# Attention scores issued as one step of four 32-row tiles into four PSUM banks, with unrolled programs and a new order of steps on every engine

## The reference, cut to what matters

```python
# layer 0: 32 heads of 16, 8 key/value heads, 128 queries and 128 keys per batch element
scores = einsum('bkgld,bksd->bkgls', q, k) * scale + mask
out = einsum('bkgls,bksd->bkgld', softmax(scores), v)
x = layernorm(out @ Wo + bo + x) * gamma + beta
# layer 1
xn = ln(x); sx = shift(xn)
xxx = tanh((xn + sx * maa_x) @ maa_w1)             # low
x5 = xn + sx * (maa_stack + xxx @ maa_w2)          # low_rank, mix: five inputs
w = exp(-exp(td + tanh(x5[1] @ decay_w1) @ decay_w2)); r, k, v, g = projections of x5
for t: out_t = r_t . (u * a_t + s);  s = a_t + w_t * s,  a_t = outer(k_t, v_t)   # 32 heads of 16x16
x = x + (groupnorm(out) * g) @ Wo.T
x = x + sigmoid(xr @ Wr.T) * (relu(xk @ Wk.T) ** 2 @ Wv.T)    # after a second ln and shift
```

## Time and profile before

| what | value |
|---|---|
| median of 3 runs | 2512.75 us (2511.68 to 2516.52) |
| the profiled execution | 2511.9 us |
| its span | 2510.1 us |
| PE busy | 2306.4 us, 92% |
| DVE busy | 2164.8 us, 86% |
| ACT busy | 942.2 us, 38% |
| POOL busy | 568.3 us, 23% |

### The profile page before, as it was taken

One profiled execution on the slowest core, in us unless ns is written; L12 is line 12 of the kernel. 1 busy time (PEld: TensorE's weight loads), 2 busy tenths in 40 slices (PEclk: granted clock), 3 DMA queues, 4 the chain that ended last, 5 costly groups with the idle time before them and its releaser, 6 DMA issues. The chain is left out here.

```text
span 2510.1 us, 43786 instructions
## 1 busy us (share of the span) xinstructions
PE 2306.4 (92%) x14144; PEld 1578.5 (63%) x14144; DVE 2164.8 (86%) x5337; ACT 942.2 (38%) x3169; POOL 568.3 (23%) x762
## 2 busy tenths in 40 slices
PE   4697999999999999999999999999999999999966
PEld 3474766667576675757657575665757666675633
DVE  1368999999989898998989889898898999999993
ACT  2434352624425252442624335262342526244111
POOL 1122223131222313122131212213122231322200
PEclk8798999999999999999999999999999999999977
DMA  7000001010000101001010100101001010100000
GB/s 249 19 10 29 1 10 37 2 46 1 19 29 10 38 1 46 1 10 38 10 37 1 39 9 10 38 10 37 1 14 34 10 37 4 44 1 20 8 17 9
DMA packets 48435, 61.86 MB, mean 25 GB/s; under 512 B 20208, under 2 KB 25968, under 8 KB 48208
## 3 DMA queue, kind: packets, MB, share of 16 engines
q1 hardware_dynamic: 48208, 58.93, 7.5%
HBM read 42.14 MB, written 16.78 MB: 23 GB/s over the span
## 5 line engine op out<-in xcount | busy, mean ns | idle before, releaser
L1140 DVE TENSOR_TENSOR_SCAN st<-ws,st 128x256 f32<-128x256 f32 x1024 | 620.5, 671 | 10.5 <-POOL st L994 10.4
L851 ACT ACTIVATE probs_or_mixes<-probs_or_mixes,least 128x128 f32<-128x128 f32 x1024 | 396.8, 397 | 25.1 <-DVE least L1087 24.6
L1150 DVE TENSOR_TENSOR st<-st,rT 128x1024 f32<-128x1024 f32 x256 | 327.5, 1280 | 19.4 <-issue 16.6
L1129 DVE TENSOR_TENSOR st<-bank_pair,kT 128x1016 f32<-128x1016 f32 x256 | 309.8, 1210 | 37.1 <-PE bank_pair L701 36.3
L1087 DVE CUSTOM_DVE_ANT_0 probs_or_mixes<-bank,nmask 128x128 f32<-128x128 f32 x1024 | 228.8, 285 | 55.8 <-PE bank L569 34.1
L1018 POOL TENSOR_TENSOR probs_or_mixes<-probs_or_mixes 128x512 f32<-128x512 f32 x160 | 187.4, 1193 | 268.0 <-DVE probs_or_mixes L1212 268.0
L1024 POOL TENSOR_TENSOR rstd<-rstd,mhalf 128x1 f32<-128x1 f32 x96 | 80.1, 835 | 701.4 <-DVE rstd L1169 701.4
L701 PE MATMUL bank_pair<-v_hi,sel 32*128 32x256 f32 x1024 | 187.3, 346 | 50.1 <-DVE st L1129 50.0
L994 POOL COPY st<-s 128x8 f32<-128x8 f32 x256 | 76.5, 312 | 646.3 <-PE bank L724 423.9
L851 ACT ACTIVATION_READ_ACCUMULATOR probs_or_mixes<-probs_or_mixes,least 128x1 f32 x1024 | 201.0, 196 | 0.0
L701 PEld LDWEIGHTS bank_pair<-v_hi,sel 32*128 32x128 f32 x1024 | 110.2, 189 | 131.3 <-DVE st L1129 70.9
(11 more groups left out here) (137 smaller groups left out, 4210.4 us busy)
## 6 DMA issues: line engine op xcount, KB each, us to landing
cin<-in_ctx SPq DMA_DIRECT2D x16, 512.0 KB, 3.7
xin<-in_x SPq DMA_DIRECT2D x16, 512.0 KB, 3.7
x<-xin SPq DMA_DIRECT2D x16, 512.0 KB, 3.7
keep<-x SPq DMA_DIRECT2D x16, 512.0 KB, 3.9
out<-keep SPq DMA_DIRECT2D x32, 256.0 KB, 2.0
wo<-in_wo SPq DMA_DIRECT2D x2, 1024.0 KB, 11.4
nmask<-in_mask SPq DMA_DIRECT2D x16, 128.0 KB, 4.5
wq<-in_wq SPq DMA_DIRECT2D x1, 1024.0 KB, 9.5
```

The lines of the kernel that those rows point to most:

```text
L851: last = fn(pr[:, n % 4, j, :], pr[:, n % 4, j, :], ACT.Exp, bias=least[:, n, j:j + 1], scale=-1.0, accum_out=rsum[:, n, j:j + 1])
L1129: tt(dst, src, over(kv, DU, 1), ALU.mult).then_inc(outer.sem, 1)
L1140: last = nc.vector.tensor_tensor_scan(v, ws[:, c].rearrange("p b t -> p (b t)"), v, 0.0, ALU.mult, ALU.add)
L1150: tt(v, v, over(rT[:, u // PER, :], DU, 1), ALU.mult).then_inc(weighed.sem, 1)
```

## The change

PE's score step now serves four tiles: it waits for the four banks of the ring at once and issues eight matmuls, four row groups in turn for each of the two column halves. DVE and ACT keep a step for each tile. The hardware loops are gone: all 18 iterations are written out on every engine. The four lists are in a new order. Instructions, their number and their sizes are the same.

```diff
@@ psum_jobs @@
         elif name == "score":
-            keys = [(name, n), (name, n + 1)]
+            keys = [(name, n + m) for m in range(4)]
@@ periods (the same on SP) @@
-            for it in range(LOOP_FROM):
-                once(it)
-            with eng.Fori(LOOP_FROM, LOOP_TO) as i:
-                once(i)
-            for it in range(LOOP_TO, G + LATEST):
+            for it in range(G + LATEST):
                 once(it)
@@ score on PE @@
+                four = range(n, n + 4)
                 hold(pe, emptied, g, *([through("key", 0)] if n == 0 else []),
-                     *([through("query", n // 4)] if n in (0, 4) else []), (("score", n), 0, 0),
-                     (("score", n + 1), 0, 0))
-                ps = {m: (bank[XB.of(("score", m))], filled[XB.of(("score", m))]) for m in (n, n + 1)}
+                     *([through("query", n // 4)] if n < 8 else []), *((("score", m), 0, 0) for m in four))
                 for ci in range(2):
-                    for m in (n, n + 1):
+                    for m in four:
+                        at = XB.of(("score", m))
                         r = slice(32 * (m % 4), 32 * (m % 4) + 32)
-                        last = mm(ps[m][0][:, ci * 2 * L:(ci + 1) * 2 * L], qT[r, 2 * cp + ci, b, :],
+                        last = mm(bank[at][:, ci * 2 * L:(ci + 1) * 2 * L], qT[r, 2 * cp + ci, b, :],
                                   kbd[r, b, :, :], start=True, stop=True)
                         if ci == 1:
-                            last.then_inc(ps[m][1], 1)
+                            last.then_inc(filled[at], 1)
@@ PE_ORDER, one line of ten @@
-low_rank.2+1 spread.14+2 tdecay.0+1 turn_c.0 proj_k.0+1 turn_c.1 spread.15+2 decay.0+1 turn_x.0 reduce.6+2 proj_v.0+1
+spread.15+2 low_rank.0+1 reduce.6+2 low_rank.2+1 proj_r.0+1 proj_k.0+1 proj_v.0+1 tdecay.0+1 turn_x.0 spread.0+1
```

More of the change, by code:

```diff
@@ new lines @@
+reduce.7+2 turn_c.0 decay.0+1 spread.1+1 mean.1+2 decay.1+1 var.0+2 turn_x.1 proj_r.1+1 turn_c.1 spread.2+1 query.0
+key.0 rstd.0+2 rstd.1+2 query.1 low_rank.4+1 spread.3+1 out.0+2 reduce.0+1 score.0 spread.4+1 out.1+2 proj_k.1+1
+proj_g.0+1 proj_g.1+1 turn_p.0 spread.5+1 turn_p.1 turn_p.2 score.4 reduce.1+1 spread.6+1 turn_m.0+2 turn_p.3 value.0
+proj_v.1+1 turn_p.4 turn_m.1+2 spread.7+1 values.0 turn_p.5 turn_p.6 turn_p.7 score.8 spread.8+1 reduce.2+1 ffn_k.0+2
+spread.9+1 values.1 flip.0 turn_p.8 turn_p.9 turn_p.10 share.0 score.12 reduce.3+1 turn_p.11 project.0 spread.10+1
@@ L130 @@
+turn_p.12 turn_p.13 values.2 ffn_k.1+2 turn_p.14 ffn_r.0+2 flip.1 turn_p.15 share.1 spread.11+1 values.3 reduce.4+1
+spread.12+1 project.1 spread.13+1 ffn_v.0+2 spread.14+1 ffn_r.1+2 turn_n.0 turn_n.1 reduce.5+1 ffn_v.1+2 mean.0+1
+low.0
 """
 ACT_ORDER = """
-turn_c.0 turn_x.0 turn_c.1 decay.0+1 proj_v.0+1 turn_x.1 proj_r.0+1 decay.1+1 mean.1+2 proj_r.1+1 query.0 key.0
-proj_g.0+1 proj_v.1+1 score.0 score.1 score.2 proj_g.1+1 query.1 turn_p.0 turn_p.1 score.3 turn_p.2 score.4 turn_p.3
-score.5 score.6 turn_p.4 turn_p.5 score.7 proj_k.1+1 turn_p.6 turn_p.7 flip.0 score.8 score.9 share.0 score.10
@@ L139 @@
+score.10 ffn_k.0+2 flip.0 turn_p.8 turn_p.9 turn_p.10 share.0 score.11 turn_p.11 score.12 score.13 score.14 score.15
+turn_p.12 ffn_k.1+2 turn_p.13 turn_p.14 flip.1 turn_p.15 ffn_r.0+2 share.1 ffn_r.1+2 turn_n.0 turn_n.1 mean.0+1 low.0
+proj_r.0
 """
 POOL_ORDER = """
-rk.0+1 first.1+1 rk.1+1 negate.0 mix.4+1 first.2+1 first.3+1 first.4+1 norm2.0+2 first.5+1 turn_x.0 first.6+1
-norm2.1+2 turn_x.1 rk.2+1 first.7+1 norm0.0 first.8+1 first.9+1 affine0.0 norm1.0 norm0.1 affine0.1 rk.3+1 first.10+1
@@ L149 @@
[L149 to L152, removed]
-score.10 score.11 scan.6+1 score.12 score.13 scan.7+1 gather.0 score.14 outer.8+1 score.15 shift2.0+2 project.0
@@ L154 @@
-inverse.1 weigh.6+1 norm0.0 weigh.7+1 scan.8+1 apply0.0 outer.9+1 gather.1 weigh.8+1 scan.9+1 norm1.0 project.1
-norm0.1 weigh.9+1 apply0.1 keep_row.0 outer.10+1 readout.1+1 apply1.0 norm1.1 outer.11+1 apply1.1 scan.10+1
-weigh.10+1 shift.0 outer.12+1 scan.11+1 scan.12+1 weigh.11+1 ffn_v.0+2 ffn_v.1+2 mix.0 mix.1 outer.13+1 mix.2 mix.3
+proj_v.0+1 weigh.15+2 outer.0+1 readout.3+2 outer.1+1 var.0+2 scan.0+1 outer.2+1 weigh.0+1 groupnorm.0+2 scan.1+1
+scan.2+1 weigh.1+1 mix.4+1 out.0+2 outer.3+1 score.0 score.1 norm2.0+2 score.2 score.3 scan.3+1 weigh.2+1 weigh.3+1
@@ new lines @@
+outer.4+1 apply2.0+2 out.1+2 scan.4+1 norm2.1+2 weigh.4+1 proj_g.0+1 proj_g.1+1 outer.5+1 apply2.1+2 score.4 score.5
+score.6 outer.6+1 score.7 scan.5+1 scan.6+1 value.0 proj_v.1+1 readout.0+1 weigh.5+1 outer.7+1 weigh.6+1 shift2.0+2
+score.8 score.9 score.10 score.11 key.0 outer.8+1 inverse.0 scan.7+1 scan.8+1 weigh.7+1 gather.0 score.12 score.13
+outer.9+1 score.14 scan.9+1 score.15 outer.10+1 project.0 readout.1+1 weigh.8+1 inverse.1 scan.10+1 norm0.0 weigh.9+1
+apply0.0 weigh.10+1 outer.11+1 gather.1 norm1.0 outer.12+1 scan.11+1 project.1 norm0.1 apply0.1 keep_row.0 apply1.0
@@ L157 @@
+outer.13+1 weigh.11+1 norm1.1 ffn_v.0+2 apply1.1 scan.12+1 shift.0 scan.13+1 readout.2+1 outer.14+1 weigh.12+1
+ffn_v.1+2 weigh.13+1 mix.0 mix.1 mix.2 mix.3 outer.15+1 scan.14+1 weigh.14+1 scan.15+1
 """
```

26 lines of the change are left out of this document (7 added, 19 removed).

## The result

The changed kernel takes 2611.64 us (median of 4 runs, 2607.55 to 2622.32), against 2513.19 us of the kernel before measured beside it: a ratio of 1.040, with a 95% interval from 1.036 to 1.043. It is slower by 4%. The forecast of 2516 us was wrong, and so was its range of 2470 to 2550: 96 us lie between forecast and result.

The account below looks back on a forecast made before the run. A closed chain between PE and DVE bounds the kernel: span 2510.1 less 48.7 for loops is 2461.4, plus 57.4 for 14 longer periods, less 4 at the end, plus 1.8 around the span: say 2516 us, range 2470 to 2550.

Parts of the forecast that it names:

- gap 1: DVE, `mix.0` to `groupnorm.0`: the way by POOL and PE takes 37.5 us, DVE's 28.9; wait 8.7 with hand-over.
- What bounds the kernel, and the loops: Closed chain between PE and DVE, 143.7 us an iteration; removing the loop saves 48.7 us, span 2510.1 to 2461.4.
- The step of four tiles: PE's score steps at 1.06 us: 4.2 us less work an iteration, cancelled by 4.1 us of waits for four banks.
- rival R4: PE's score steps: the four tiles don't overlap, a step takes 2.1 us, period 148.8, about 2530 us; chance 0.10.
- gap 2: DVE, `project.0` to `project.1`: PE's 16 steps take 23.4 us, DVE's work 21.6 to 22.5; wait taken as 1.1.
- gap 3: DVE, `apply0.1` directly after `norm0.1`: POOL's power between them is uncovered, 0.7 us with two hand-overs.
- The period: One iteration: DVE's own work 137.3 + 8.7 + 1.1 + 0.7 = 147.8 us against 143.7, uncertain by 1.3.
- the end: Last group's way from `mix.0` to `scan.0`: from 37.2 us to about 33, so 4 us less.
- R3: PE's clock falls after waits before `low_rank.0` and `proj_r.0`; period 1.5 to 2.5 us longer, 2535 to 2560; chance 0.14.
- the ring rule: At `project.0` on PE: the step takes the bank of `score.13`, which DVE empties; used in gap 2.

Follow-up runs that it names:

- pairs: Changed kernel with each four-tile score step written as two two-tile steps, plus the fillers: 2536.08 us; the same without the fillers: 2587.13 us.
- the one test of gap 1: Kernel with the fillers plus 4 more unused matmuls on PE ahead of `tdecay.0`, where PE doesn't wait: 2580.97 us, against 2554.96 without.
- the fillers: Changed kernel plus unused matmuls on PE: 6 ahead of `ffn_k.0`, 4 of `spread.14`, 3 of `low_rank.0`, 2 of `proj_r.0`: 2554.96 us, ratio 1.017.

## Why the prediction was wrong

The way from before to after, in medians: the loops -47 (2511.95 to 2464.71), the new order with pairs and hardly any step at the lower clock +71 (2536.08), the step of four instead of pairs +19 (2554.96), the clock in the waits +57 (2611.64). The medians come from three series, in which the kernel before took 2511.95, 2512.25 and 2515.82 us, so each part is known to a few us. The 71 are what is left beside the parts that were undone: no run takes the new order away alone, and their reading by gaps below rests on the traces and on the one test of gap 1.

*What bounds the kernel, and the loops:* right. 48.7 us were forecast.

*The step of four tiles:* half right. It takes 1.15 us, as taken from the earlier trace rows; rival R4 falls. The waits are 0.86 at `score.4`, 1.73 at `score.8`, 0.78 at `score.12`, none at `score.0`: 3.4 us where 4.1 stood. The Trainium skill says in TensorEngine Tiling (Array Packing), section PSUM Bottleneck, that tiling speeds up TensorE but not the emptying of PSUM. The traces agree: the step takes 1.15 us where two pairs took 1.76 at `score.4`, and it ends no earlier than they do. What failed is the sentence that places where PE waits "cost nothing, as long as PE's 139.2 stays under it". They cost 19 us: the first tile of four comes 0.7 us later, and behind the wait `reduce.2` ran at the lower clock in seven groups.

*Gap 1:* right. The way from the first operation of `mix.0` to the second of `groupnorm.0` takes 37.7 us with the fillers (1315.60 to 1353.31), where 37.5 were forecast. In the iteration with fillers shown above DVE waits 0.50 + 0.75 + 0.20 + 1.34 + 1.50 + 1.48 + 0.18 (the last is the second operation of `groupnorm.0`), 5.95 us, and `scan.14` takes 4.46 us instead of the 2.43 of the earlier trace rows, `weigh.15` 1.7 instead of 1.2: 8.5 us against the 8.7 forecast. Some 2.5 us of it are longer operations, where the forecast had only waits.

*Gaps 2 and 3:* right in size; gap 2 is 1.00 + 0.37 at two `outer` steps and not at `project.1` (forecast 1.1), gap 3 is 0.66 (0.7). For gap 2 that is partly luck: the terms listed for DVE add up to 21.5 to 21.8 us and not to 22.5, so by them the wait would have been 1.6 to 1.9.

*The period:* 148.5 with the full clock and pairs, against 147.8; the miss of 0.7 is within the 1.3 allowed. The small waits that I hadn't listed (`score.0` 0.4, `apply0.0` 0.44, `shift.0` 0.44) are 1.3 us, so something else came out smaller. The order alone makes 2536 us with pairs, 20 more than I had for order and step together. In the profiled executions that is 3 us from the kernel without loops (a span of 2464.3, not 2461.4), 14 from a period that grew by 5.1 us and not by 4.1, and 3.6 in the first period (138.5 against 134.9 us without loops), for which the sum had no term; the end got shorter by 2.8 us and not by 4, and group 0 reached `shift.0` 2.7 us sooner, which the sum didn't have either.

*R3:* the mechanism that decided, and the step that failed. The sum put the clock behind PE's waits at nothing; it was only a rival with a chance of 0.14, and it cost 57 of the 96 us. Three things were wrong in R3 itself. Its price was too low: 2 us a period, where the clock made 4.6 to 5.2 us (154.4 against 149.8 in the mean with fillers, against 149.2 in their clean iterations). For its own place the price was about right: where `proj_r.0` alone was slow, three of four periods were about 1.5 us longer. Its places were too few: more of the gain came from `ffn_k.0` and `spread.14` than from the two I named. I had seen the wait at `spread.14` and called it free, and I had missed that of 3.08 us at `ffn_k.0`, which takes the bank of `score.8`, which DVE empties only behind its 4.5 us of `shift2.0`; the ring rule that I used for `project.0` would have given it. And the evidence against it was taken from the wrong row. A piece of 0.93 us at a clock of 1.00 says nothing on pieces of 1.4 to 3.1 us. The same iteration had one of 1.67 us at a clock of 1.00, ahead of the same `ffn_r.1`, which the reading left out, and in two of the eleven groups with such a piece the lower clock followed; for longer ones there was the piece of 2.87 us with 0.57 behind it. These rows have both levels behind waits of this size, so the clock belonged in the sum, as a price times how often it would fall. The Trainium skill, TensorE: Matmul & The Clock Gate, Part 1, calls the throttled state the default, which activity releases. The fillers agree with it: the kernel got faster by unused matmuls, 2611.64 to 2554.96 us.

*The range:* the forecast of 2516 lacked 20 us for the order, 19 for the step of four and 57 for the clock, which make 2612. The upper end of 2550 gave all three together 34, since each stood as a rival to the others and none as a term of the sum, though they can all be true at once.
